# A scan's output product in twelve float32r passes: high and low parts on three engines, five rows parked in memory

## The reference

```python
Y = (Yd + Yo).transpose(0, 1, 3, 2, 4).reshape(B, L, H, P)
Y = Y + D[:, None] * xh
y = Y.reshape(B, L, D_INNER) * silu(z)
return y @ w_out.T            # y: 2048 x 512, w_out: 512 x 512, float32
...
h = res + mamba2(...)         # then rmsnorm, the gated MLP, the layer again
```

## Time and profile before

| | |
|---|---|
| median of 3 runs | 764.51 us (764.18 to 764.58) |
| the profiled execution | 763.5 us |
| its span | 761.7 us |
| TensorE busy | 747.7 us (98%) |
| VectorE, ScalarE, GpSimd busy | 629.8, 447.3, 336.6 us |
| granted TensorE clock | full over the whole span |

### The profile page before, as it was taken

How to read it: one execution, slowest core, us unless ns; L and a number is a source line. 1 busy time by engine, 2 the same in 40 slices (tenths; PEclk the granted TensorE clock), 3 DMA queues, 4 the chain that set the end, 5 groups by cost and what they waited for, 6 DMA issues and landing times.

```text
span 761.7 us, 10468 instructions
## 1 busy us (share of the span) xinstructions
PE 747.7 (98%) x3360; PEld 348.6 (46%) x3360; DVE 629.8 (83%) x1237; ACT 447.3 (59%) x877; POOL 336.6 (44%) x391
## 2 busy tenths in 40 slices
PE   8999999999999999999999999999999999999998
PEld 3444444455444544444444444444444444444444
DVE  7798888878878979968799978878878878767994
ACT  4867868677786585543645556456456456444441
POOL 5631535654352289765414343243243243224584
PEclk9999999999999999999999999999999999999999
DMA  8933645563331134220521733733733733443565
GB/s 300 198 75 80 163 93 108 124 113 71 79 88 34 37 57 116 63 56 1 134 44 23 175 70 69 166 70 70 165 70 70 163 72 68 78 77 70 114 161 154
DMA packets 97413, 75.03 MB, mean 98 GB/s; under 512 B 65504, under 2 KB 72992, under 8 KB 97360
## 3 DMA queue, kind: packets, MB, share of 16 engines
q0 software_dynamic: 17280, 31.46, 23.1%
q1 hardware_dynamic: 77872, 39.70, 20.4%
q10 hardware_dynamic: 2208, 3.21, 1.7%
HBM read 23.46 MB, written 4.23 MB: 36 GB/s over the span
## 4 chain that ended last, share of the span: by engine, by line
PE 62%; DVE 22%; ACT 7%; issue 5%; POOL 2%; DMA 2%; ACTq 0%; SPq 0%; DVEq 0%; POOLq 0%
PE PS L2034 57%; DVE raw L1506 3%; PE PS L2158 2%; DVE stage L1506 2%; PE PS L2166 1%; DVE st L1338 1%; DVE state L1488 1%; DVE w_in L1611 1%; DMA x_t<-hb 1%; DVE S L1471 1%; DVE h2n_p L1429 1%; DVE xs L1435 1%; ACT pre L924 1%; DVE wv L1462 1%; ACT th L940 1%
## 5 line engine op out<-in xcount | busy, mean ns | idle before, releaser
L735 POOL DMA_DIRECT2D xs<-x x59 | 50.9, 863 | 153.8 <-ACT x L1204 139.5
L2034 PE MATMUL PS<-h,w_in 128*128 128x512 f16 x480 | 108.7, 379 | 0.5 <-DMA h<-hn_p 0.5
L2034 PE MATMUL PS<-h,x_t 128*128 128x512 f16 x408 | 94.0, 379 | 0.0
L2034 PEld LDWEIGHTS PS<-h,w_in 128*128 128x128 f16 x480 | 46.9, 98 | 65.6 <-issue 15.5
L2034 PE MATMUL PS<-n_T,stage 128*128 128x512 f16 x288 | 71.5, 379 | 0.0
L1204 ACT ACTIVATE x<-PS,d_d 128x512 f32<-128x512 f32 x59 | 40.3, 682 | 39.0 <-PE PS L2034 39.0
L2034 PEld LDWEIGHTS PS<-h,x_t 128*128 128x128 f16 x408 | 39.5, 98 | 48.1 <-issue 2.2
L545 POOL TENSOR_TENSOR r<-mv,mhalf 128x1 f32<-128x1 f32 (+1 forms) x32 | 29.6, 925 | 64.7 <-DVE mv L1342 51.3
L735 POOL DMA_DIRECT2D xs<-n x29 | 25.2, 869 | 67.0 <-ACT n L1204 56.7
L2034 PE MATMUL PS<-pre,stage 128*128 128x512 f16 x192 | 49.3, 379 | 0.0
L1174 ACT ACTIVATE xds<-tm,dgh 128x512 f32<-128x512 f32 x24 | 17.3, 722 | 53.8 <-DVE tm L1958 53.8
(11 more groups left out here) (326 smaller groups left out, 1811.4 us busy)
## 6 DMA issues: line engine op xcount, KB each, us to landing
xs<-x POOLq DMA_DIRECT2D x75, 256.0 KB, 3.3
xs<-n POOLq DMA_DIRECT2D x29, 256.0 KB, 3.3
x_t<-x_in SPq DMA_DIRECT2D x16, 256.0 KB, 3.4
x_t<-hb POOLq DMA_DIRECT2D x16, 256.0 KB, 4.4
out<-x_t SPq DMA_DIRECT2D x15, 256.0 KB, 2.3
raw_gu<-gate_t SPq DMA_DIRECT2D x7, 512.0 KB, 4.3
raw_gu<-up_t SPq DMA_DIRECT2D x7, 512.0 KB, 6.5
raw_d<-down_t SPq DMA_DIRECT2D x7, 512.0 KB, 7.3
```

Source lines behind the costliest of these rows:

```text
L735: po.dma_start(chunk_of(xs, c), d_tmps[d % 3], accum_op=ALU.add).then_inc(s_acc[d % 3], 16)
L2034: ins = pe.matmul(out_, lhs(a, b, k), rhs(a, b, k), start=first and n == 0, stop=last and n == len(todo) - 1)
```

## The change

`w(c)` computes the same product from parts of type float32r: y = y_hi + y_lo and w_out = w_hi + w_lo, and the sum of y_hi w_hi, y_hi w_lo and y_lo w_hi, four products each, 12 in all. For this:

- ScalarE makes `y_hi` (`high_y`), behind `gate_y(c)`, at one of three places in its step (`HIGH_FIRST`, the default, `HIGH_LATE`), and `w_out_hi` in the prologue in two pieces;
- GpSimd makes `y_lo` (`low_y`) of 12 rows, between `scan_c(c+1)` and `scan_d(c+1)`; VectorE makes that of the rows 11, 12, 13 and 15 (`LO_DVE`), and `w_out_lo` in the prologue in four pieces;
- in the steps with j = 1 and 3 of the first three stages (`W_LATE`) TensorE does the second slot's product before `w(c)`, not after it;
- VectorE does `gate_y(13)`, `weights(14)` and `scan1(14)` at the end of step 12, with `dn_lo(0)` behind `gate_lo`; and `gate_y(15)` at the end of step 14, ahead of `t_los(1, ...)`;
- the parts need room: `xs` keeps 11 rows, and a row c uses `c % 11`. The rows 0 to 4 are stored to memory by SP's queue (`park(c)`, in SP's steps 2 to 6, between `t2` and `t1`), VectorE's x1 statistics of the rows 11 to 15 wait for that, and one DMA of ScalarE brings all five back after the last `w`; VectorE's `down(0)` waits for it.

```diff
+        w_out_lo = under("w_out_lo", [P, H, DM])
         w_out = sb("w_out", [P, H, DM])
...
-        xs = sb("xs", [P, NCH, DM])
+        xs = sb("xs", [P, NCH - N_PARK, DM])
+        split = under("split", [P, N_PARK, DM])
+        xl = sb("xl", [P, N_PARK, DM])
+        w_out_hi, y_hi = split[:, 0:H, :], split[:, H, :].rearrange("p (h q) -> p h q", h=H)
...
+        LO_DVE = (11, 12, 13, 15)
...
+        W_LATE = (1, 3)
...
+            def park(c):
+                sp_.wait_ge(*x2_added(c))
+                sp_.dma_start(x_park[c, :, :], row(c)).then_inc(s_park, 16)
...
+            def low_y(c):
+                po.wait_ge(e_y_hi, c + 1)
+                y, lo_ = y_of(c)
+                po.tensor_tensor(lo_, y, y_hi, ALU.subtract).then_inc(e_y_lo, 1)
...
                     if c != 2 * CH + 3:
                         scan_c(c + 1, (c + 1) % CH)
+                    if c not in LO_DVE:
+                        low_y(c)
                     scan_d(c + 1, (c + 1) % CH)
...
+            def high_w_out(n):
+                ac.wait_ge(s_wout, 16)
+                ac.activation(w_out_hi[:, 2 * n:2 * n + 2, :], w_out[:, 2 * n:2 * n + 2, :], ACT.Copy).then_inc(e_wr_hi, 1)
+
+            def high_y(c):
+                ac.wait_ge(e_y, c + 1)
+                if c > 0:
+                    ac.wait_ge(e_wo, c)
+                ac.activation(y_hi, y_of(c)[0], ACT.Copy).then_inc(e_y_hi, 1)
...
+            HIGH_FIRST = (2 * CH + 2, 2 * CH + 3, NCH - 1)
+            HIGH_LATE = (0, 1, 3, 4, 5, 13, 14)
...
+            ac.wait_ge(e_wo, NCH)
+            ac.dma_start(xl[:, :, :], x_park.rearrange("c p n -> p c n")).then_inc(s_back, 16)
...
                 if c == 3 * CH:
-                    cut_b()
+                    gate_y(c + 1, j + 1)
+                    cut_b_gu()
+                    weights(c + 2, j + 2)
+                    scan1(c + 2, j + 2)
+                    low_y(c + 1)
...
                 if c == 3 * CH + 2:
+                    gate_y(c + 1, j + 1)
                     t_los(1, 0, 1, 2, 3)
...
-                pe.wait_ge(e_y, c + 1)
+                pe.wait_ge(e_y_hi, c + 1)
                 pe.wait_ge(*freed)
                 for h in range(H):
-                    last = pe.matmul(bank(b), y[:, h, (c % CH) * P:(c % CH + 1) * P], w_out[:, h, :], start=h == 0, stop=h == H - 1)
+                    pe.matmul(bank(b), y_hi[:, h, :], w_out_hi[:, h, :], start=h == 0, stop=False)
+                if c == 0:
+                    pe.wait_ge(e_wr_lo, H)
+                for h in range(H):
+                    pe.matmul(bank(b), y_hi[:, h, :], w_out_lo[:, h, :], start=False, stop=False)
+                pe.wait_ge(e_y_lo, c + 1)
+                for h in range(H):
+                    last = pe.matmul(bank(b), y_of(c)[1][:, h, :], w_out_hi[:, h, :], start=False, stop=h == H - 1)
                 last.then_inc(e_wo, 1)
...
+                if i + 1 < NS and j in W_LATE:
+                    proj(i + 1, SLOTS[j][1])
                 w(c)
```

More of the change, by code:

```diff
@@ L58, in sem, with under @@
             return ctx.enter_context(nc.semaphore(name))
+        def under(name, shape):
+            with nc.sbuf_tensor(name, shape, F32R) as t:
+                return t
         w_ffn = [sb(f"w_ffn{p}", [P, KB, DM], F16) for p in range(2)]
         w_in = [sb(f"w_in{p}", [P, KB, NPROJ], F16) for p in range(2)]
+        w_out_lo = under("w_out_lo", [P, H, DM])
         w_out = sb("w_out", [P, H, DM])
@@ L75, in build @@
                     for b, n in ((0, CB), (CB, ZB)))
+        y_lo = [t[:, CB * ST:(CB + ZB) * ST].rearrange("p (b t) -> p b t", b=ZB) for t in (stage_r, raw_r)]
         def gated_home(t):
@@ L100, in build @@
         tm = sb("tm", [P, 2, 2, P])
-        with nc.sbuf_tensor("idle_r", [P, DM], F32R) as t:
-            idle_r = t
+        idle_r = under("idle_r", [P, DM])
         Ld = sb("Ld", [P, H, P])
@@ L249, in heads, with row, end_row, y_of @@
             return PS[:, b, :].rearrange("p (h q) -> p h q", h=H)
[L251 to L252 removed]
+        def row(c):
+            return xs[:, c % (NCH - N_PARK), :]
+        def end_row(c):
+            return xl[:, c, :] if c < N_PARK else row(c)
+        LO_DVE = (11, 12, 13, 15)
+        def y_of(c):
+            cols = slice((c % CH) * P, (c % CH + 1) * P)
+            return szs[(c // CH) % 2][:, :, cols], y_lo[(c // CH) % 2][:, :, cols]
         def tokens_of(t, c):
@@ L325, in build @@
                 put(("gu", j, 1), (e_gated, j + 1), B_P[1])
+            if i + 1 < NS and j in W_LATE:
+                put_proj(i + 1, SLOTS[j][1])
             put(("w", c), (e_x2, c + 1), None if i + 1 < NS else B_P[2])
-            if i + 1 < NS:
+            if i + 1 < NS and j not in W_LATE:
                 for q in SLOTS[j][1:]:
@@ L808, in hi1 @@
                 for dst in (hn_of(c), hn_parts(c)[:, 0, :]):
-                    last = ac.activation(dst, chunk_of(xs, c), ACT.Identity, scale=r1[:, c, 1:2], bias=b1[:, c, 1:2])
+                    last = ac.activation(dst, row(c), ACT.Identity, scale=r1[:, c, 1:2], bias=b1[:, c, 1:2])
                 last.then_inc(e_hn_hi, 1)
@@ L979, in step @@
                     slot_b(i_late, late[0])
+                if c not in HIGH_FIRST and c not in HIGH_LATE:
+                    high_y(c)
                 if a + 1 < NCH:
@@ L1754, in step @@
                     advance(c, j)
-                if c + 1 < NCH:
+                if c == 3 * CH:
+                    low_y(c)
+                if c + 1 < NCH and c != 3 * CH + 1:
                     if c + 2 < NCH:
```

70 lines of the change are left out of this document (49 added, 21 removed).

## The result

The changed kernel takes 783.80 us (median of 4 runs, 781.56 to 785.53), the kernel before 764.48 beside it: the ratio is 1.0252 with a 95% interval of 1.0226 to 1.0278, 19.3 us slower. The forecast was 769.0 with a range of 759.5 to 773.0. Its direction was right; the loss is four times the 4.5 us of its sum. The profiled execution took 783.73 us with a span of 782.0 (761.7 before).

What follows compares the result with a forecast made beforehand. The scan is bound by a chain through VectorE, ScalarE and GpSimd, not by TensorE's 98% busy time. Terms -0.1 + 1.4 + 1.5 + 3.0 - 1.3 = +4.5 us gave 769.0 us against the median, range 759.5 to 773.

Steps and rivals of the forecast that it cites:

- three signs of being wrong: No wait at `w(2)`, a float32r pass over 0.25 us, or VectorE's two-input instructions in rows 8 to 10 no longer.
- faster rival: Pieces on VectorE, ScalarE and GpSimd fall into waits: 760.2 us, holding if `residual2(3)` starts before 151.6 us; chance 0.26.
- The passes: In `w`, twelve float32r passes at 0.23 us apiece: 0.7 to 0.75 us less a row, 3.0 us at four places.
- GpSimd's low parts, rows 2 and 6: `y_lo` comes late behind `scan_c`; TensorE stands 3.7 us in `w(2)`; costs 1.4 us at row 3, 1.5 from row 6.
- Row 6 repeats it ... 1.5 us: At `w(6)` the late low part of row 2 recurs: 220.0 against 218.52 us, 1.5 us on the chain.
- ScalarE's high part: `high_y`: nothing in rows 0, 1, 3, 4, 5, 13, 14; 0.5 us each in rows 8, 11, 12.
- GpSimd's low parts and VectorE: GpSimd's added 1.27 us a row holds up VectorE: 0.5, 0.8 and 0.3 us in rows 8, 9 and 10.
- VectorE's low parts: Subtractions cost 0.68 us, 0.6 in sequence; those of y in rows 11, 12, 13 and 15 said to be counted below.
- Late gates, -1.3: Rows 13 and 15: plus 0.6 us for `low_y(13)`, -1.9 at row 15 with the gate ahead of `t_los`; together -1.3.
- Prologue, -0.1: Last low part of `w_out` delays S of row 0 by about 0.65 us, using up `w(0)`'s saving: -0.1 for both.
- Parking, nothing: Five rows out by SP's queue and back before `down(0)`: nothing, with 6.6 us as upper bound.
- The rival with GpSimd at every row (777.5): GpSimd blocks VectorE at eight of rows 0 to 10 at 1.27 us: 10.2 in place of 1.6 us; chance 0.06.

Runs made afterwards that it cites:

- Twelve passes: Kernel before with parking and twelve float32r products a row in place of four float32 ones, no splitting: 762.92 us, ratio 0.9980.
- four passes: Kernel before with parking and one group of four float32r products a row, no low parts: 761.87 us, ratio 0.9976.
- the fill: Changed kernel, with TensorE repeating products in `w(2)` and `w(6)` until the late low part comes: 780.42 us, ratio 1.0216.
- the low part made sooner: Changed kernel, with GpSimd making the low parts of rows 2 and 6 before `ln1_chain`: 779.44 us, ratio 1.0205.
- the run with the gates back: Changed kernel with the old order of the late gates, `cut_b` whole, `low_y(13)` on VectorE behind the advance: 783.64 us, ratio 1.0257.

## Why the prediction was wrong, step by step

The runs divide the 19.3 us so (differences of medians, each uncertain by about 2 us): passes -1.6; high parts 5.0; the low part of `w_out` and the two orders together 1.3 (taken out where no low part of y is waited for); VectorE's low parts of y 5.7; GpSimd's 4.5; their place in rows 2 and 6 4.4. In ratios to the kernel before, which take out the difference between chips, the same steps are -1.8, 5.6, 0.5, 6.0, 5.0 and 3.6 us. The steps that failed are named below: row 6, the high parts, VectorE's low parts and the late gates, and a clock that no term had. The forecast had one or two for most of them. None of its three signs of being wrong showed (the wait at `w(2)` was there, a pass took 0.23 us, VectorE's instructions with two inputs in SBUF were longer), and the start of `residual2(3)` at 156.6 us ruled out its faster rival, as it said; so the signs covered the mechanisms it had and not those it lacked.

- *The bound.* Right: the chain is VectorE's and ScalarE's, and the sum by TensorE's busy time was to be left alone. Twelve passes bring 1.6 us and four passes not clearly more, though TensorE does 29 us less.
- *The passes.* The pace was right: a row of twelve takes 2.8 us where nothing waits, 0.23 apiece. The 3.0 us at four places were 1.4 to 1.6: rows 3 and 4 stood on the chain only by tenths of a microsecond.
- *GpSimd's low parts, rows 2 and 6.* The waits (3.7 us twice) and the wait of `residual2(3)` (2.48 for 2.6) came as worked out, and row 3 cost 1.35 us for 1.4. That this agrees is luck: with the S(0) shift taken off, VectorE came 2.6 us later there than forecast, mostly by ScalarE's high part of row 2, and TensorE's stretch to `w(3)` took 1.7 us more, at the lower clock; and of the 1.35 us the fill took back 1.0. The step that failed is the next sentence, "Row 6 repeats it ... 1.5 us". The step there is 4.3 us, 3.3 more than with the low part made sooner, for two reasons. The first consumer behind `w(6)` is not `residual2(7)` but the gate of row 7, which from step 7 on stands in the middle of the step, 11.1 us sooner on VectorE than its residual (207.41 against 218.52 before), and it had no slack; it waited 4.78 us. And the term has no line for the clock. The fill shows that the clock is 3.5 of the 5.0 us of both rows together; the wait alone cost 0.4 us at row 3 and 0.5 at row 6, and the rest of its 1.5 us came only at S(11). So the forecast had the wait dearer at these rows than it was, and the clock at nothing.
- *ScalarE's high part.* "In rows 0, 1, 3, 4, 5, 13 and 14 ... nothing. In rows 8, 11 and 12 ... 0.5 us each" leaves out rows 2, 6, 7, 9, 10 and 15, whose high part stands ahead of `hi1` or `hi2`. The whole was 5.0 us, not 1.4: 1.9 at row 2 and 1.05 at row 7 alone. A pass of 0.54 us costs its own length, and the wait for its input (0.59 us at row 2) in an engine that goes in order, and what the later start then meets (0.76 us beside GpSimd).
- *GpSimd's low parts and VectorE.* 1.6 us by the forecast, 4.0 to 4.5 by leaving them out. The mechanism was right; at row 9 it fell on a 16-column operation (1.24 us for 0.17) and not on the tap. At rows 9 and 10 it held up VectorE by 1.1 us each where the forecast took 0.8 and 0.3, and the clock's share had no line. Three rows at the full 1.27 us, as in the upper bound, are 3.8 us, less than the run showed.
- *VectorE's low parts.* The forecast says that the four of y are "counted below", but the sum has 0.6 for row 13 and 0.7 for row 15 and nothing for rows 11 and 12 (they appear only in the upper bound, as "two of 0.6"), without a reason; row 11 alone cost 1.6 us. "0.6 in sequence" was read from an instruction with one input in PSUM. These have two in SBUF and took 1.01, 0.72, 2.82 and 1.79 us in the stretch where GpSimd makes the MLP's sums, and cost 5.7 us in all. This is the term that was missed by most, and the trace of before had it: the subtractions of 128x512 behind 286 us take up to 2.5 us there.

```profile
322.96 2.54 DVE L1611 TENSOR_TENSOR w_in<-hn_p,w_in 128x512 f16<-128x512 f32 x1
```

- *Late gates, -1.3.* Nothing, by the run with the gates back. The gate of row 15 goes ahead of `t_los`, but `low_y(15)` is issued in step 15, behind them: it starts 4.2 us after the gate's end (341.1 to 345.3) and takes 1.79 us. The forecast's path, gate, low part, four products, is not the one that runs: in TensorE's list the 24 products of `gate_up` stand before `w(15)`, which begins at 345.14 and ends at 348.4, 7.3 us behind the gate, and no wait shows in it. `residual2(15)` does not wait for it either, where it waited 1.63 us before; it starts at 349.94, behind VectorE's own row of work.
- *Prologue, -0.1.* 0.5 us: 0.9 for the low part of `w_out`, whose last two pieces took 1.13 and 1.16 us, less 0.4 at `w(0)`.
- *Parking, nothing.* Right.
- *"Behind 330 us ... the shift carries through".* Right: the 20 us of shift at the first MLP products are there at the end.

The range failed because its ends added each piece by its own bound and had none for the pieces that were missing. The rival with GpSimd at every row (777.5) was the nearest, given 0.06; its upper end of 1.27 us a row was near for rows 9 and 10. What is left open: how the 8 us between S(8) and S(13) divide when the pieces act together, since the clock, GpSimd's hold and the high part raise each other there, and the runs take them out in one order only.

## What to carry to other kernels

A new wait of TensorE can cost more than it lasts (here 3.5 us for the clock and 1.5 for the wait): price the work behind it at half pace as well, and look for the first consumer in the list of each engine, step by step, not by the name of the row before. A small operation that is inserted into an in-order queue costs its length, the wait for its own input, and what the later start meets; where the queue feeds the chain, the sum of many such pieces, each "half a microsecond in a wait", is what decides. An engine that shows 98% busy may be following: taking 12 us off it was worth 1.6 us here, so try the saving alone, with the new operations left out, before building what pays for it.
